# A graph layer on one core: where TensorE does the sums of four blocks of edges

## The reference

```python
h = relu(layernorm(x))
e = concat(h[src], h[dst])                       # row, col of the edge_index
g1 = lrelu(einsum('ef,hgf->heg', e, gate_w1))    # 4 heads x 64
a = node_vec[col] * exp(lrelu(g1 . gate_w2))     # one weight per head and edge
m1 = lrelu(einsum('ef,hgf->heg', e, msg_w1))     # 4 heads x 128
beta = lrelu(einsum('heg,hog->heo', m1, msg_w2)) # 4 heads x 64
# per node: sum over its edges of a * beta, divided by the sum of a, mean over the heads
x = x + layer0
```

## Time and profile before

| | |
|---|---|
| median of three runs | 6132.26 us (6117.36 to 6136.0) |
| the profiled execution | 6118.99 us, span 6116.3 us |
| TensorE matmuls | 4418.4 us busy, 72% of the span, 25058 records |
| VectorE | 4662.3 us, 76% |
| ScalarE | 2592.6 us, 42% |
| GpSimd | 3568.6 us, 58% |
| mean granted clock of TensorE | 0.794 of 2.4 GHz |

### The profile page before, as it was taken

How to read it: one execution, slowest core, us unless ns; L and a number is a source line. 1 busy time by engine, 2 the same in 40 slices (tenths; PEclk the granted TensorE clock), 3 DMA queues, 4 the chain that set the end, 5 groups by cost and what they waited for, 6 DMA issues and landing times.

```text
span 6116.3 us, 108132 instructions
## 1 busy us (share of the span) xinstructions
PE 4418.4 (72%) x25058; PEld 2776.0 (45%) x25058; DVE 4662.3 (76%) x10241; ACT 2592.6 (42%) x6354; POOL 3568.6 (58%) x3639
## 2 busy tenths in 40 slices
PE   5799999999999999999999933344444444444444
PEld 4555555555555555555555513333333333333333
DVE  3488888888888888888888866667766676676675
ACT  3677776767776767767677640000000000000000
POOL 0255655555556556556555536566666666666665
PEclk9999999999999999999999965555555555555555
DMA  8533333333333333333333342222222222222221
GB/s 215 190 75 77 76 77 75 78 75 77 76 75 78 74 77 77 75 76 76 77 75 77 74 123 44 44 46 45 47 47 46 46 46 50 45 46 45 49 46 34
DMA packets 324279, 435.66 MB, mean 71 GB/s; under 512 B 132852, under 2 KB 204756, under 8 KB 323068
## 3 DMA queue, kind: packets, MB, share of 16 engines
q0 software_dynamic: 122512, 173.81, 16.4%
q1 hardware_dynamic: 188284, 250.00, 13.9%
q10 hardware_dynamic: 13296, 9.92, 0.9%
HBM read 362.45 MB, written 70.96 MB: 71 GB/s over the span
## 4 chain that ended last, share of the span: by engine, by line
PE 38%; DVE 32%; issue 12%; another core or an unknown queue 12%; ACT 3%; DMA 1%; DVEq 1%; ACTq 0%; POOL 0%; SPq 0%; POOLq 0%
PE ps_beta L1937 11%; PE ps_hidden L1885 8%; PE ps_hidden L1886 6%; DVE dots L1761 4%; DVE work L1333 4%; PE ps_beta L1945 3%; PE ps_sum L1956 3%; DVE table_sb L1640 3%; DVE work L1755 3%; DVE centered L1640 3%; DVE work L1794 2%; DVE work L1800 2%; PE ps_alpha L1919 2%; DVE equal L1787 2%
## 5 line engine op out<-in xcount | busy, mean ns | idle before, releaser
L786 POOL DMA_INDIRECT ends<-split_table,parts x1612 | 1581.0, 981 | 1532.9 <-issue 1399.2
L1885 PE MATMUL ps_hidden<-ends_parts,w_high 128*128 128x512 f32 x2418 | 1094.9, 453 | 114.4 <-DVE work L1333 65.7
L839 POOL DMA_INDIRECT work<-src_table,parts x808 | 805.5, 997 | 601.0 <-DVE work L1800 308.4
L1333 DVE TENSOR_TENSOR work<-work,ps_hidden 128x512 f32<-128x512 f32 x1612 | 1102.7, 684 | 15.2 <-ACT work L923 2.4
L923 ACT ACTIVATE work<-ps_hidden 128x512 f32<-128x512 f32 x1612 | 955.7, 601 | 143.8 <-PE ps_hidden L1886 102.5
L839 POOL DMA_INDIRECT ends<-src_table,parts x804 | 813.0, 1011 | 313.4 <-issue 240.6
L1886 PE MATMUL ps_hidden<-ends_hot,window 128*128 128x512 f32 x2418 | 955.5, 395 | 0.0
L2143 PE MATMUL ps_beta<-work,equal 128*128 128x128 f32 x1616 | 413.9, 437 | 729.2 <-DVE work L1800 577.6
L1338 DVE TENSOR_TENSOR beta<-beta_scaled,ps_beta 128x512 f32<-128x512 f32 x806 | 552.2, 685 | 412.4 <-ACT beta_scaled L981 349.8
L1126 ACT ACTIVATE ps_alpha<-dots 128x8 f32<-128x8 f32 x403 | 72.0, 179 | 1841.8 <-DVE dots L1761 1156.8
L1937 PE MATMUL ps_beta<-work,msg_w_sb 128*64 128x512 f32 x3224 | 825.0, 611 | 3.9 <-DVE work L1333 0.2
(11 more groups left out here) (220 smaller groups left out, 6713.5 us busy)
## 6 DMA issues: line engine op xcount, KB each, us to landing
window<-window_table SPq DMA_DIRECT2D x403, 192.5 KB
parts<-in_edge_attr SPq DMA_DIRECT2D x101, 512.0 KB
dst_rows_sb<-in_dst_rows SPq DMA_DIRECT2D x403, 128.0 KB
ends<-split_table,parts POOLq DMA_INDIRECT x1612
window_table<-parts SPq DMA_DIRECT2D x49, 386.0 KB
sums<-key_rows POOLq DMA_DIRECT2D x403, 32.6 KB
work<-src_table,parts POOLq DMA_INDIRECT x808
ends<-src_table,parts POOLq DMA_INDIRECT x804
```

The costliest lines, as they stand in the source:

```text
L786: pool.indirect_dma_start(out=ends[m][:, t, :], out_offset=None, in_=split_table, in_offset=bass.IndirectOffsetOnAxis(ap=src_all[:, b * T ...
L839: pool.indirect_dma_start(out=ends1_windows[m][:, t, :], out_offset=None, in_=src_table, in_offset=bass.IndirectOffsetOnAxis(ap=src_all[:, ...
L1333: nc.vector.tensor_tensor(hidden[k][:, :], scaled[k % NL][:, :], ps_hidden[k % NL][:, :], ALU.max).then_inc(hidden_ready, 1)
L1885: nc.tensor.matmul(o, w1_high[:, k * P:(k + 1) * P], ends_parts[j][:, :], start=True, stop=False)
```

## The change

The 16 matmuls of `sum_quad` become four rounds, one per edge tile t, each with the four blocks m side by side. Round 0 stands behind product 0 of block b + 1, round 1 behind its product 1, round 2 behind pair product 0 and round 3 behind pair product 1. The three waits stand ahead of round 0, the update of `summed` behind round 3. The last quad's rounds come one behind the other at the end, as before.

```diff
-            def sum_quad(b, quad):
-
-                pe.wait_ge(terms_ready, 2 * b + 2)
-                pe.wait_ge(src_hot_ready, b + 1)
-                wait(pe, quad_copied, quad)
-                for t in range(T):
-                    for m in range(last_m(quad) + 1):
-                        last = nc.tensor.matmul(ps_sum[m * WIN0:(m + 1) * WIN0, 0:W0], hot_quad[m][:, t, :].bitcast(F32),
-                                                terms_quad[m][:, t, :], start=(t == 0), stop=(t == T - 1))
-                last.then_inc(summed, 1)
+            def sum_round(b, quad, t):
+
+                if t == 0:
+                    pe.wait_ge(terms_ready, 2 * b + 2)
+                    pe.wait_ge(src_hot_ready, b + 1)
+                    wait(pe, quad_copied, quad)
+                for m in range(last_m(quad) + 1):
+                    last = nc.tensor.matmul(ps_sum[m * WIN0:(m + 1) * WIN0, 0:W0], hot_quad[m][:, t, :].bitcast(F32),
+                                            terms_quad[m][:, t, :], start=(t == 0), stop=(t == T - 1))
+                if t == T - 1:
+                    last.then_inc(summed, 1)
...
+                sums = m == 0 and begun
                 first_product_windows(b, 5, half, j)
                 if not is_final(b):
                     first_product_windows(b + 1, 0, half + j, 1 - j)
+                if sums:
+                    sum_round(b - 1, quad - 1, 0)
+                if not is_final(b):
                     first_product_windows(b + 1, 1, half + j, 1 - j)
+                if sums:
+                    sum_round(b - 1, quad - 1, 1)
                 turn_gates(b)
                 pair_product(b, 0)
-                if m == 0 and begun:
-                    sum_quad(b - 1, quad - 1)
+                if sums:
+                    sum_round(b - 1, quad - 1, 2)
                 pair_product(b, 1)
+                if sums:
+                    sum_round(b - 1, quad - 1, 3)
...
-            sum_quad(NBW - 1, NQ - 1)
+            for t in range(T):
+                sum_round(NBW - 1, NQ - 1, t)
```

## The result

The changed kernel takes 6339.14 us (median of 4 runs, 6332.51 to 6348.79), the kernel before beside it 6132.08 (6117.36 to 6136.0): ratio 1.0341, 95% interval 1.0328 to 1.0354. The change costs 207 us, where 90 were forecast. The profiled execution has a span of 6340.2 us; the first layer is still clocked at 1.00, as before.

A forecast was written before the change was run, and what follows sets the result against it. In the first layer TensorE was busy 3225 of 3330 us, VectorE 2877. Per quad + 1.34 + 0.66 - 1.10 = + 0.90 us; 100 quads give 90 us, taking the median 6132.26 to 6222 us, range 6136 to 6268.

The forecast's parts named there:

- Step (1): Ahead of product 1: round 0 waits for VectorE's second weighing of the quad's last block, 1.34 us of new idle.
- Step (2): Product 1 to round 3: one piece becomes four, each paying for width changes; 5.36 us instead of 4.70, 0.66 more.
- The 0.07 and 0.06: Amounts in us added to product 1 (0.65 in all) and to turn_gates (0.37 in all) between rounds.
- The change of 0.14: Cross-check on TensorE: one width change takes 0.14 us, so nine instead of four would add 0.7.
- the rival with wait and widths both small: Round 0's wait: second weighing done some 0.5 us earlier in most quads; 6132 to 6142 us, no change; chance 0.08.
- Step (3): Blocks m = 1 and m = 2: VectorE and ScalarE work in the gap; m = 1 gives back 1.10 us, m = 2 nothing.
- The give-back of 1.10: Block m = 1 no longer waits ahead of product 0 and runs in 7.11 to 7.2 us instead of 8.23.
- the late signal is the whole price: Pair 1's late completion follows 32 matmuls in one piece; single rounds avoid it: -0.46 us a quad, 6086 us; chance 0.10.
- Each round has a late signal of its own: Or pays its change twice: another 0.3 to 0.5 us a quad through pairs 0 and 1; 6252 to 6272; chance 0.12.
- wrong if: Signs: round 0 within 0.3 of product 0's end, a round under 0.5, or the m = 1 block above 7.8.
- the list of what was to be seen: Profile after: round 0 idle some 1.3, m = 0 near 11.6, m = 1 near 7.15, m = 2 and 3 unchanged, rounds 0.58.

The follow-up runs named there:

- the early piece: The kernel before with all four rounds of the sums in one piece behind product 0, ahead of product 1; 5809.19 us, ratio 1.030.

## Why the prediction was wrong

**Step (1), the wait: right.** Forecast 1.34; round 0 starts 6.18 into the block where 6.23 was worked out, and without the wait m = 0 is 1.20 shorter. The idle ahead of it is 1.14 in the trace, because that is counted from product 0's modelled end, 5.05 into the block, and the forecast counted from 4.89, where product 1 used to start.

**Step (2), the pieces: right.** Forecast 0.66; every round takes the 0.58 taken from the gate product's row, and 0.75 is left in m = 0 when the wait is gone. The 0.07 and 0.06 added to product 1 and to the gates came from no row, but the two were measured at 0.66 and 0.37 where 0.65 and 0.37 were forecast. (The change of 0.14 worked out beside the sum from 1.90 and 0.57 is 0.13, and the rival with wait and widths both small takes 0.5 from 0.29 and keeps 0.0 to 0.1, which does not follow; the forecast uses neither.) The two steps together were to make m = 0 longer by 2.00, and it is 1.97 (1.73 where the gathers are left out).

**Step (3) failed, in its last clause: "The m = 2 block begins as every block does that follows two pair products in one piece, waiting for chunk 1, so nothing more comes back".** The give-back of 1.10 in m = 1 came, as 0.90 in the mean. But m = 2 took 1.18, where 0 was forecast. The sum for a quad is +2.14 (with m = 3's -0.11) and not +0.90, and 1.24 x 100 = 124 us is the size of the gap of 117. And a sentence further up, "no DMA; nothing on SP's or POOL's queue moves", holds for the lists of instructions but not for their times: the batch of m = 1 starts 1.1 later in the quad (16.09 against 14.97, medians), and the loads move from ahead of it to behind its start.

The fault behind it: the 1.12 by which m = 1 stood above 7.11 was read as a payment for the sums, which ends when the sums move. The runs without gathers show m = 1 at 7.10 in the old order and in the new; there is nothing in the order to be given back. What was read there is a cost that comes with the gathers. Without them the change costs 1.74 a quad (31.75 to 33.49) on chips 13 and 2. With them each kernel pays about the same on top, in other places: on chip 2 before 32.77 - 31.75 = 1.02, after 34.53 - 33.49 = 1.04; in the first profiles 1.20 and 1.60. With hindsight the sum is 1.74 + 0 to 0.4, 174 to 214 us, and 173 (chip 2) and 207 were measured, with 178 and 183 where the gathers are left out (chips 2 and 13).

Of the rivals, "the late signal is the whole price" blamed the sums in one piece. Its doubt was the right one (nothing in the profile explained 2.34 against 1.20), its cause was not: in one piece and without gathers the signal takes 1.13. "Each round has a late signal of its own" saw lateness reach VectorE through pairs 0 and 1, and that did happen: pair 0 was late in 68 of 99 quads and pair 1 in 57. But it is not a matter of the rounds, since none was late without the gathers and one in 99 without the loads, and its 0.3 to 0.5 a quad falls short. What was named as "wrong if" did not come about (round 0 started well behind product 0, a round took 0.58, m = 1 stayed under 7.8), so those signs would have passed a wrong forecast; m = 2 unchanged, in the list of what was to be seen, was the one that failed.

**Left open:** by what mechanism the signals are held back, and whether GpSimd's work on the gathers or their transfers do it (leaving them out takes away both); whether four in a run matter; whether the place of the loads or only their presence counts; why chip 13 has none of it; and why the same chip had the kernel before at 6070 us in one group of runs and at 6130 in another. Which of the two loads matters was not tried.

**A version that beats both, by 0.2%:** the sums in one piece behind both pair products, 0.9976 (0.9965 to 0.9988) on chip 2, and 0.9977 (0.9964 to 0.9989) on chip 8. It has one width change less and adds no wait, but m = 0 is not shorter for it (9.61 against 9.59); the gain is what m = 1 gives back and m = 2 does not take. It ran only on chips with late signals.

## What to carry to other kernels

When a block is longer than its work explains, ask whether that time belongs to the order or to what is in flight beside it before counting on getting it back: a piece of time that nothing in the profile explains can move to the next place instead of going away. Moving a reader of freshly made data earlier in an in-order queue costs the whole wait and everything behind it (on chip 13 the early piece alone costs 1.65 of the 1.74 a quad); spreading it in pieces costs 0.14 to 0.15 for each width change. Count what the queues of the loads do too: a new order moves them in time even when no DMA is touched, and here m = 2 was not hit once they were left out. And look whether a hold that is put in has held anything: three runs here had a wait that was already met, for every batch or for the one that mattered.

## What the runs showed of the hardware

- TensorE's signals arrive late around gathers, on chips 2, 4 and 8 and in the first two profiles. Pair 1 took 2.34 us from its start to ScalarE with four gathers in a row and 1.13 without; product 3 took 2.1 instead of 0.46; with six gathers and an add in a row, pair 0 took 6.5. In these the release came 1.2, 1.1 and 0.7 us after the last of them had ended on GpSimd; but without SyncE's loads the same batch delayed nothing in m = 2. On chip 13 blocks with gathers took the same 7.11 and 7.53 as without.
- Where signals are late the trace also holds fewer records of them: of the semaphore that counts the 2418 products of the first layer, the trace of the kernel before has 1630 updates, against 2418 without gathers on chip 2 and 2378 and 2377 with gathers on chip 13. Releasers named "issue" or "remote" in such traces are to be read with care.
- What a round pays for standing alone: 0.58 against 0.475 in one piece, in the changed kernel and without its wait. One width change more cost a block 0.14, five cost it 0.75.
- Chips differ by far more than this change: the kernel before took 5641 us on chip 13 and 6070 to 6132 elsewhere. Without gathers in the first layer its blocks are alike to 0.01 us on chips 13 and 2, so the 368 us between 5637.78 and 6006.16 lie outside the blocks of the first layer: from 3560 us to the end the two traces take 2070 and 2452 us.
